# Gathered rows of a graph kernel: SyncE moves one tile in 64, row by row, in place of GpSimd

## The reference, cut to what matters

```python
f0, f1 = fctp_scalar(x0, x1, node_attr, W_l1_0, W_l1_1, MUL)
g0 = f0[edge_src]
g1 = f1[edge_src]
...
outA = wA * g0 * e0
outB = wB * jnp.einsum('euk,ek->eu', g1, e1) / SQRT3
outC = (wC * g0)[..., None] * e1[:, None, :]
outD = wD[..., None] * g1 * e0[..., None]
seg = lambda v: jax.ops.segment_sum(v, edge_dst, num_segments=n)
```

## Time and profile before

| | |
|---|---|
| median of 3 runs | 7861.12 us (7858.62 to 7862.42) |
| the profiled execution: its own time | 7861.93 us |
| the profiled execution: its span | 7859.9 us |
| first and last `t_ge` (L1776), start | 3812.0 and 7817.9 us |
| GpSimd busy, whole span | 3320.6 us (42%), of it 3048.4 us in L1566 |

### The profile page before, as it was taken

One profiled execution on the slowest core, in us unless ns is written; L12 is line 12 of the kernel. 1 busy time (PEld: TensorE's weight loads), 2 busy tenths in 40 slices (PEclk: granted clock), 3 DMA queues, 4 the chain that ended last, 5 costly groups with the idle time before them and its releaser, 6 DMA issues.

```text
span 7859.9 us, 124589 instructions
## 1 busy us (share of the span) xinstructions
PE 6932.2 (88%) x37774; PEld 5697.3 (72%) x37775; DVE 4864.2 (62%) x9083; ACT 3889.0 (49%) x7386; POOL 3320.6 (42%) x3464
## 2 busy tenths in 40 slices
PE   6999996999997999998788888888888888888887
PEld 4666664888886788886677777777777777777776
DVE  9999996333333333334666666666666666666665
ACT  6999995666664666665322222222222222222222
POOL 2111110000001000001577777777777777777775
PEclk9999998999998999999877787777777777777777
DMA  4666666555554555555433333333333333333332
GB/s 89 137 139 139 141 139 156 153 145 145 145 145 127 152 145 145 145 145 146 125 86 84 88 84 87 86 84 87 86 86 86 87 85 88 84 87 86 84 88 60
DMA packets 624603, 884.18 MB, mean 112 GB/s; under 512 B 198493, under 2 KB 512316, under 8 KB 618064
## 3 DMA queue, kind: packets, MB, share of 16 engines
q1 hardware_dynamic: 483980, 490.53, 21.9%
q0 software_dynamic: 114320, 377.25, 20.5%
q10 hardware_dynamic: 26036, 12.80, 0.6%
HBM read 684.41 MB, written 195.81 MB: 112 GB/s over the span
## 4 chain that ended last, share of the span: by engine, by line
POOL 33%; issue 12%; DMA 3%; DVE 2%; POOLq 1%; DVEq 1%; SPq 0%; PE 0%; ACT 0%; ACTq 0%
POOL t_rows L1566 33%; DMA t_rows<-table,t_ends 2%; DMA t_attrs<-in_edge_attr 1%; DVE t_msg_ad L1780 1%; DVE t_msg_bc L1794 0%; POOLq L173 0%; DVE t_cg L1779 0%; SPq L1538 0%; DVE t_msg_ad L1782 0%; POOLq L1564 0%; DVE t_ge L1776 0%; DVE t_rel L1867 0%; DVE acc L1757 0%; DVE t_msg_bc L1789 0%; DVEq L1878 0%
## 5 line engine op out<-in xcount | busy, mean ns | idle before, releaser
L1566 POOL DMA_INDIRECT t_rows<-table,t_ends x3224 | 3048.4, 946 | 1008.6 <-issue 966.2
L1587 ACT ACTIVATE t_weight<-t_weight,t_attrs 128x64 f32<-128x64 f32 x3224 | 691.9, 302 | 2662.3 <-PE t_weight L1666 2628.2
L937 ACT ACTIVATE c_wide_act<-c_raw 128x1024 fp32r<-128x1024 uint8 (+1 forms) x1400 | 1457.4, 1043 | 648.6 <-PE c_sums L1011 641.5
L1702 PEld LDWEIGHTS t_sums<-t_hot,t_msg_ad 128*128 128x128 f32 x6464 | 969.3, 235 | 916.9 <-issue 916.4
L992 DVE CAST c_wide_dve<-c_raw 128x1024 fp32r<-128x1024 uint8 (+1 forms) x1400 | 770.6, 552 | 1353.8 <-PE c_sums L1011 1353.2
L1011 PE MATMUL c_sums<-c_wide_act,c_parts 128*128 128x512 f32 (+1 forms) x5600 | 1485.1, 387 | 70.1 <-DVE c_parts L976 60.9
L1702 PE MATMUL t_sums<-t_hot,t_msg_ad 128*128 x6464 | 1000.2, 321 | 615.9 <-DVE t_hot L1874 615.5
L1011 PEld LDWEIGHTS c_sums<-c_wide_act,c_parts 128*128 128x128 f32 x5600 | 1044.2, 189 | 290.6 <-issue 80.5
L1011 PE MATMUL c_sums<-c_wide_dve,c_parts 128*128 128x512 f32 (+1 forms) x4200 | 1169.1, 387 | 0.0
L705 ACT ACTIVATE a_a_sb<-a_sums 128x784 bf16<-128x784 f32 x1568 | 1140.6, 941 | 25.2 <-PE a_sums L672 24.7
L1776 DVE TENSOR_TENSOR t_ge<-t_rows,t_edge 128x768 f32<-128x768 f32 x403 | 384.4, 954 | 1204.3 <-DMA t_rows<-table,t_ends 1191.0
(11 more groups left out here) (203 smaller groups left out, 5225.9 us busy)
## 6 DMA issues: line engine op xcount, KB each, us to landing
c_raw<-a_dram SPq DMA_DIRECT2D x672, 448.0 KB, 3.4
a_dram<-a_a_sb POOLq DMA_DIRECT2D x49, 3136.0 KB, 18.2
t_scal<-in_edge_attr SPq DMA_DIRECT2D x403, 256.0 KB
t_rows<-table,t_ends POOLq DMA_INDIRECT x3224
t_ends<-in_edges SPq DMA_DIRECT2D x403, 8.0 KB
t_attrs<-in_edge_attr SPq DMA_DIRECT2D x403, 16.0 KB
c_raw<-a_dram SPq DMA_DIRECT2D x28, 224.0 KB, 2.5
table<-n_out SPq DMA_DIRECT2D x24, 256.0 KB, 2.3
```

The source lines that it names most:

```text
L937: act.activation(to, of, ACT.Copy).then_inc(act_wide, 1)
L1566: pool.indirect_dma_start(out=rows[:, slot, t, :], out_offset=None, in_=table, in_offset=bass.IndirectOffsetOnAxis(ap=ends[:, slot, t:t + ...
L1587: mul = act.activation(ad, ad, ACT.Copy, scale=attrs[:, slot, t, 0:1])
L1702: pe.matmul(sums[:, of, 0:WIDE], msg_ad[:, slot % 2, t, :], hot[:, of, t, :], start=t == 0, stop=t == T - 1)
```

## The change

In every round from 1 to 49, for slot 0 only, GpSimd leaves out the last of the 8 tiles: 49 indirect DMAs fewer. SyncE fetches the 128 rows of that tile instead, one DMA per row. The host gives it the source numbers of these tiles in an array of their own, `picks`, one line of 128 per round; SyncE loads the line of the next round in the body of slot 7. It reads the numbers into registers four at a time, and each number is the address of one row's DMA. The 128 rows are spread over the bodies of slots 0 to 6, in `PICKED`: 18, 18, 18, 19, 18, 18 and 19 rows, each set with a semaphore of its own. The rows of round r are issued in the bodies of round r, so after group 8r - 8 has been counted, and VectorE waits for all seven semaphores ahead of `t_ge` of group 8r. `gathered` only adapts the counts of `rows_landed`.

```diff
+PICKED = [range(P * k // 7, P * (k + 1) // 7) for k in range(7)]
+AT_ONCE = 4
...
+        def picked(slot, r):
+
+            return slot == 0 and (not isinstance(r, int) or 1 <= r < ROUNDS)
+
+        def gathered(slot, r):
+
+            if slot > 0:
+                return r * (16 * T) + 16 * T
+            return r * (16 * (T - 1)) + 16 * T + (16 if isinstance(r, int) and r == ROUNDS else 0)
...
+                def load_picks(r):
+                    sp.dma_start(picks_of[:], picks[bass.ds(r, 1), :]).then_inc(picks_landed, 16)
+
+                def pick_rows(slot, r):
+
+                    if slot == 0:
+                        due = worked_out(sp, picks_reg, r * 16)
+                        sp.wait_ge(picks_landed, 16)
+                        sp.wait_ge(picks_landed, due)
+                    if slot < len(PICKED):
+                        for k, p in enumerate(PICKED[slot]):
+                            if k % AT_ONCE == 0:
+                                few = min(AT_ONCE, PICKED[slot].stop - p)
+                                sp.load(some[0:few], picks_of[0:1, p:p + few])
+                            row = sp.snap(some[k % AT_ONCE], min_val=0, max_val=N - 1)
+                            sp.dma_start(rows[p:p + 1, 0, T - 1, :], table[bass.ds(row, 1), :]
+                                         ).then_inc(picked_landed[slot], 16)
...
                     if i is not None and slot == 6:
                         load_nodes(i, i, FULL)
+                    if picked(0, r):
+                        pick_rows(slot, r)
+                    if slot == SLOTS - 1:
+                        load_picks(r + 1)
...
-                    for t in range(T):
+                    for t in range(T - 1 if picked(slot, r) else T):
...
-                    dve.wait_ge(rows_landed[slot], r * (16 * T) + 16 * T)
+                    dve.wait_ge(rows_landed[slot], gathered(slot, r))
+                    if picked(slot, r):
+                        for k, some in enumerate(PICKED):
+                            dve.wait_ge(picked_landed[k], r * (16 * len(some)))
...
+    picks = np.concatenate([src_groups[0:ROUNDS * SLOTS:SLOTS, :, T - 1], src_groups[:1, :, T - 1]])
```

More of the change, by code:

```diff
@@ L1418, in _, with product_edges @@
                 staged_steps(dve, [residual, normalise])
-def product_edges(nc, c, table, edges, attr, scalars, acc, x1_dram, skip_dram, out_dram):
+def product_edges(nc, c, table, edges, picks, attr, scalars, acc, x1_dram, skip_dram, out_dram):
     ctx = ExitStack()
@@ L1466, in product_edges @@
         in_time = sb("in_time", [P, 1])
+        picks_of = sb("picks", [1, P], I32)
         sums = ps("sums", (P, 2, 512))
@@ L1475, in product_edges @@
         rows_landed = [sem(f"rows_landed{i}") for i in range(SLOTS)]
+        picks_landed = sem("picks_landed")
+        picked_landed = [sem(f"picked_landed{k}") for k in range(len(PICKED))]
         groups_past, cleared, rel_ready, hot_ready, sums_ready, sums_added = [
@@ L1517, in _ @@
                 past_reg, landed_reg = sp.alloc_register("t_sp_past"), sp.alloc_register("t_sp_landed")
+                picks_reg = sp.alloc_register("t_sp_picks")
+                some = [sp.alloc_register(f"t_sp_pick{i}") for i in range(AT_ONCE)]
+                def load_picks(r):
[13 more added lines that the diff above has]
+                                         ).then_inc(picked_landed[slot], 16)
                 def load_nodes(i, n, blocks):
@@ L1530, in body @@
                         past = worked_out(sp, past_reg, g - (SLOTS - 1))
-                        landed = worked_out(sp, landed_reg, r * (16 * T))
+                        landed = worked_out(sp, landed_reg, gathered(slot, r - 1))
                         sp.wait_ge(layer1_ready, past)
@@ L1546, in body @@
                         load_nodes(i, i, FULL)
+                    if picked(0, r):
+                        pick_rows(slot, r)
+                    if slot == SLOTS - 1:
+                        load_picks(r + 1)
                 split_rounds(sp, body)
+                sp.wait_ge(picks_landed, ROUNDS * 16)
                 nth = last_steps(sp, "sp", load_nodes)
@@ L1900, in _, with gnn_kernel @@
                 last_steps(dve, "dve", step)
-def gnn_kernel(nc, x, edges, pairs_of_edges, coarse, fine, dst_groups, attr, scalars, node_vec, w, out):
+def gnn_kernel(nc, x, picks, edges, pairs_of_edges, coarse, fine, dst_groups, attr, scalars, node_vec, w, out):
     def dram(name, shape, dt=F32):
@@ L1957, in gnn_kernel @@
         with nc.sbuf_tensor("acc_2", [D, 2, NB + 1, P], F32) as acc:
-            product_edges(nc, c, table_2, edges, attr, scalars, acc, x1_dram, skip_dram, out)
+            product_edges(nc, c, table_2, edges, picks, attr, scalars, acc, x1_dram, skip_dram, out)
 WEIGHTS = ["L0_gnn_W1", "L0_gnn_b1", "L0_gnn_W2", "L0_gnn_b2", "L1_gnn_W_sc0", "L1_gnn_W_sc1", "L1_gnn_W_l1_0",
@@ L1998 @@
     edges_d = given("edges", edges)
+    picks_d = given("picks", picks)
     pairs_d = given("pairs_of_edges", pairs_of_edges)
@@ L2009 @@
     out = nc.dram_tensor("out_0", [N, D], F32, kind="ExternalOutput").ap()
-    gnn_kernel(nc, x, edges_d, pairs_d, coarse_d, fine_d, dst_d, attr, scalars, node_vec, w, out)
+    gnn_kernel(nc, x, picks_d, edges_d, pairs_d, coarse_d, fine_d, dst_d, attr, scalars, node_vec, w, out)
     result = run_bass_kernel_spmd(nc, [arrays], core_ids=[0])
```

## The result

| | before | after |
|---|---|---|
| median of 4 runs, us | 7861.17 (7858.62 to 7862.42) | 9350.62 (9348.66 to 9352.64) |
| after / before, 95% interval | | 1.1895 [1.1875, 1.1916] |
| one round of eight groups, us | 80.0 | 110.6 |
| longest wait of VectorE in a round, us | | 42.6 to 50.7, mean 45.6 |

The change costs 1489 us, where 595 us were forecast. The time lies above the range that was given (8190 to 8800).

A forecast was written before the change was run, and what follows sets the result against it. GpSimd, issuing an indirect DMA every 1.25 us, was taken to bound the kernel. After the change SyncE's closed chain, 84.0 + 2.0 + 6.1 = 92.1 us per round, would add 595 us to 7861.9: 8457 us, range 8190 to 8800.

The forecast's parts named there:

- the 61 us saved: On GpSimd: 49 indirect DMAs fewer at 1.25 us each, no part of the forecast difference since GpSimd is no longer pace.
- the other loads, `t_x`, `t_skip`: On SyncE's queue: the three loads of each of seven groups, 11.4 us per round, plus 1.25 us for `t_x` and `t_skip`.
- landing: After the last row's issue on SyncE: 2.0 us until it lands, taken from SyncE's small loads (1.6 to 2.6).
- turn of the chain: From SyncE's rows through landing and VectorE's group to the next `t_ends`: 84.0 + 2.0 + 6.1 = 92.1 us, nothing overlapping.
- Register loads: On SyncE's queue: 35 loads per round at 0.40 us and a gap of 0.04, 15.4 us; bounds 13.0 and 17.9.
- Row price: On SyncE's queue: 0.195 us around the DMA plus 0.242 for its issue, 0.437 us per row, 55.9 us for 128.
- Rival 2: On SyncE's queue: a one-row issue costs what a 128-row issue costs, 0.333 us; 9028 us, chance 0.09.
- Rival 1: SyncE's turn stays under GpSimd's 78.7 us, so all 61 us are gained; 7801 us, chance 0.05.
- Rival 3: On SyncE's queue: register loads cost 0.547 us each, 8709 us; by the skill's floor 8800; chance 0.09.
- Rival 4: The chain is not closed and only SyncE's own round counts, 87.4 us; 8227 us, chance 0.05.
- The last ten groups: End of the stage, `t_ge` of group 392 to group 402: ten groups at 8.8 us, 88 us.
- the stall: On VectorE, ahead of slot 0 in each round: some 20 us, with eight groups at 8.8 us taking 70 us.

The follow-up runs named there:

- experiment 3: The changed kernel without its register loads: four registers set once, so SyncE fetches the same four rows again and again; 7804.13 us, ratio to before 0.9927.
- experiment 4: Changed kernel's 35 loads per round without its row DMAs, GpSimd fetching all tiles; first form's loads were dropped by the build (7861.03 us), second form's kept by additions: 7860.9 us.
- experiment 8: Changed kernel with SyncE fetching 96 rows in aligned sets, ScalarE 32, and GpSimd fetching group 400's last tile in its place; 7801.51 us, ratio to before 0.9921.

## Why the prediction was wrong

**The mechanism held.** The chain is closed, SyncE's queue is on it, GpSimd is not the pace, and none of the 61 us saved counts. Term by term, per round:

| term | predicted, us | measured, us |
|---|---|---|
| rows, 128 x pitch | 55.9 (0.437) | 55.5 (0.433, the mean without loads, experiment 3) |
| register loads and what they add to the rows | 15.4 | 33.7 (103.2 - 69.5; their own time 32.6) |
| the other loads, `t_x`, `t_skip` | 12.65 | 14.0, the rest |
| first `t_ends` to end of last row | 84.0 | 103.2 |
| landing | 2.0 | 1.27 |
| VectorE's group to the next `t_ends` | 6.1 | 6.12 |
| turn of the chain | 92.1 | 110.6 |

**The step that failed is "Register loads".** It took 0.40 us for a load of four, from the bounds 0.332 and 0.474, and a load took 0.93 us in the mean, 1.07 in the median. The term is short by 18.3 us of the 18.5 by which the turn was short; the other terms' errors (-0.4, +1.3, -0.7) cancel, which is luck. The two bounds were not bounds. The 202 loads of 0.332 us on which the step leaned had no DMA ahead of them on TensorE's queue, and they were aligned: the kernel takes them from `c.bounds[0:1, bass.ds(g * 2, 4)]` with an even g, so from a multiple of four numbers. By experiment 4 they read like aligned ones (0.30 us alone). Neither holds for most of the new loads: 0.30 + 0.57 off the boundary + 0.26 behind row DMAs = 1.13. Two signs were there before the run. The cut of 128 by 7 was in the diff and put five of seven sets off the boundary, where no row had tried a load of four, and in the earlier trace rows two registers took 0.547 us where four took 0.332, so the time did not follow the count.

**Row price**: right. 0.242 us was taken for the issue and 0.228 measured; the pitch is 0.42 us in the median and 0.433 to 0.447 in the mean, since some rows, those right behind a load above all, start later. Rival 2 (0.333) is ruled out. One issue is short beside the 1.27 us to its landing, yet 128 of them, one behind another, are 55.5 us of the turn. **Landing** was 0.7 us too long, counted from the end of the issue.

**Rival 1** (SyncE keeps up, 7801) is false of the change, but experiments 3 and 8 reach its time to within 4 us. It set the deciding row price at 0.33 us with the loads at 15.4; without loads the limit is (78.7 - 8.1 - 11.4 - 1.25) / 128 = 0.45 us, and 0.433 is under it.

**Rival 3** (loads dear) named the right term and had too small a price. The floor of 600 ns in the Trainium skill, "DMA: Bandwidth & Descriptors", section "Latency and other measured facts", gave 8800, nearer than the forecast. The runs don't bear it out as a floor: aligned loads take 0.30 us alone and 0.556 behind row DMAs, both under it, and an unaligned one takes 1.12, nearly twice as much. **Rival 4** (chain not closed) is ruled out: the next row goes out only after the landing and VectorE's group, and the turn has both in it.

**The last ten groups**: 88 us forecast, 9304.4 - 9227.1 = 77.3 measured. GpSimd had run ahead (32 indirect DMAs were left for these ten groups, of 80), and groups passed faster. Likewise the stall: groups took (110.6 - 45) / 8 = 8.2 us, not 8.8, so VectorE stalled 45 us instead of 20, of which 18.5 are the longer turn. 3812.0 + 49 x 110.57 + 77.3 = 9307.2 for `t_ge` of group 402, against 9304.4. **GpSimd** is at 54% in the stretch and not 65%, with the longer turn; waits for `t_ends` or `t_attrs` to land were hardly seen there (1.2 us in 400), its free time is put down to "issue". **TensorE** idled more and its granted clock fell from 0.79 to 0.70. That cost the turn nothing: VectorE's group kept its 6.1 us, and the other seven were done 45 us before the rows came. The seven waits on VectorE's queue cost nothing visible: the landing of 1.27 us has them in it.

**The range** was too narrow for one reason: it took 0.33 to 0.47 us for a load that no row showed in its place, on that engine, at those addresses. (Its lower bound was also added up 0.4 us too low: rows at 0.42 and loads at 0.37 with the rest make 87.1 and not 86.7, some 20 us of time, which decides nothing.)

## To carry over

Price an added instruction by a row with the same engine, the same operands and the same neighbours; where none exists, such rows are examples and no bounds, and the range must say so. When SyncE loads registers from SBUF, load whole 16-byte pieces from a 16-byte boundary, many at a time. Work taken from the pacing engine is worth its full time only if whoever takes it stays under the pace for the whole turn of the chain, landing and consumer's group with it: here one queue with 128 rows and their loads was 8 to 35 us per round too long, and two queues with 96 and 32 were not.

## What the runs showed that was not expected

- SyncE's register loads cost as if 16 aligned bytes were read at a time: 0.30 us for the first 16 alone, and 0.205 for each further 16, worked out from the one larger size that was run. Off the boundary, or with fewer than four numbers, each number more costs 0.2 us: loads of 2, 3 and 4 numbers took 0.467, 0.667 and 0.867 us in the second form of experiment 4. Two numbers from a boundary took 0.470 there, so a short last load of a set gains nothing by its start.
- Behind row DMAs on the same queue a load takes 0.26 us more (0.556 instead of 0.30, 1.12 instead of 0.867). Why is left open. The DMA directly ahead doesn't decide it: behind `t_ends` and `t_attrs` alone a load took 0.30 or 0.87 us, and behind `t_x` and `t_skip` as well 1.12, while the same first load of slot 1 took 1.07 in the changed kernel, with 18 row DMAs shortly before. The number of DMAs issued shortly before would fit; no run varies it by itself. Open, too, is why the first load of a round, aligned and with no row ahead of it, takes 0.475.
- GpSimd's indirect DMA costs nearly the same for 32 rows (0.867 us) as for 128 (0.944).
- A DMA of one row is issued in 0.228 us on SyncE and 0.234 on ScalarE. ScalarE issued 32 of them per round, and VectorE waited 30 us more for it in 3000, which cost the kernel nothing.
